# Routed slots in halves of 64: 36 token tiles in place of 39, three of them shared by two experts each

## What is computed

```python
def _swiglu(x, wg, wu, wd):                      # width 256 -> 512 -> 256
    return jax.nn.silu(x @ wg.T) * (x @ wu.T) @ wd.T
shared_out = _swiglu(x, shared_gate, shared_up, shared_down)
logits = x @ gate_w.T
top_id = jnp.argmax(logits, axis=-1)
score = jax.nn.sigmoid(jnp.max(logits, axis=-1))
xs = x * score[:, None]
def body(acc, ws):
    wg, wu, wd, e = ws
    xe = jnp.where((top_id == e)[:, None], xs, 0.0)
    return (acc + _swiglu(xe, wg, wu, wd), None)
...
x = x + 0.5 * ffn(layernorm(x))
x = x + attention(layernorm(x))
x = x + 0.5 * ffn(layernorm(x))
```

## Time and profile before

| | us |
|---|---|
| median of 3 runs | 1135.99 |
| lowest, highest | 1130.5, 1139.51 |
| the profiled execution, its own time | 1137.43 |
| its span, first to last instruction | 1135.5 |
| TensorE busy in it | 1096.2 |

### The profile page before, as it was taken

One profiled execution on the slowest core, in us unless ns is written; L12 is line 12 of the kernel. 1 busy time (PEld: TensorE's weight loads), 2 busy tenths in 40 slices (PEclk: granted clock), 3 DMA queues, 4 the chain that ended last, 5 costly groups with the idle time before them and its releaser, 6 DMA issues.

```text
span 1135.5 us, 30299 instructions
## 1 busy us (share of the span) xinstructions
PE 1096.2 (97%) x11410; PEld 891.7 (79%) x11411; DVE 764.8 (67%) x1411; ACT 582.7 (51%) x961; POOL 550.8 (49%) x764
## 2 busy tenths in 40 slices
PE   8999999999999889999999999989999999999997
PEld 6788888888888767677777777768888888888886
DVE  5736656767677487868878878755447477677674
ACT  4344336666666345555555555243433256666663
POOL 5720644676666553444543541327202726566664
PEclk8999999999999989999999999999999999999999
DMA  7273134222211220000000000105241232122220
GB/s 259 74 292 117 37 116 173 66 67 71 66 61 45 65 89 3 3 3 3 3 3 3 3 3 3 39 3 212 101 152 38 102 140 68 62 67 62 71 65 14
DMA packets 39472, 80.25 MB, mean 71 GB/s; under 512 B 6452, under 2 KB 31159, under 8 KB 38336
## 3 DMA queue, kind: packets, MB, share of 16 engines
q1 hardware_dynamic: 27568, 52.94, 12.9%
q0 software_dynamic: 11232, 25.20, 7.1%
q10 hardware_dynamic: 560, 0.52, 0.1%
HBM read 57.13 MB, written 27.00 MB: 74 GB/s over the span
## 4 chain that ended last, share of the span: by engine, by line
PE 80%; DVE 11%; ACT 4%; issue 2%; POOL 1%; DMA 1%; ACTq 0%; DVEq 0%; SPq 0%; POOLq 0%
PE PS L1851 19%; PE PS L1765 13%; PE PS L1865 12%; PE PS L1781 8%; PE PS L1858 3%; PE PS L1939 3%; PE PS L1696 2%; DVE A_NM L801 2%; PE PS L2059 2%; PE PS L1799 2%; PE PS L2072 2%; DVE A_NM L808 1%; ACT XNT L1272 1%; PE PS L1792 1%; PE PS L2010 1%
## 5 line engine op out<-in xcount | busy, mean ns | idle before, releaser
L1851 PE MATMUL PS<-WHL,XGH 128*128 128x512 f32 x624 | 217.5, 430 | 0.6 <-DVE WHL L682 0.6
L1865 PE MATMUL PS<-WD,XNT 128*128 x624 | 149.5, 382 | 1.5 <-ACT XNT L1191 1.5
L703 DVE SCALAR_TENSOR_TENSOR XNT<-PS,SCORES,XNT 128x512 f32<-128x512 f32 x78 | 58.6, 751 | 117.4 <-PE PS L1851 117.4
L1599 POOL TENSOR_TENSOR A_W<-A_XC,CB 128x256 f32<-128x256 f32 x86 | 61.7, 737 | 151.4 <-DVE A_XC L906 151.4
L1186 ACT ACTIVATE XNT<-PS,SCORES 128x512 f32<-128x512 f32 x78 | 53.8, 690 | 145.2 <-PE PS L1851 145.0
L1851 PEld LDWEIGHTS PS<-WHL,XGH 128*128 128x128 f32 x624 | 111.4, 189 | 18.8 <-DVE WHL L682 1.1
L1865 PEld LDWEIGHTS PS<-WD,XNT 128*128 128x128 f32 x624 | 112.6, 190 | 15.6 <-issue 2.0
L1506 POOL DMA_INDIRECT X<-xs_dram,WHO x78 | 96.5, 1238 | 57.6 <-issue 23.1
L1851 PE MATMUL PS<-WHL,XGL 128*128 128x512 f32 x312 | 123.2, 395 | 0.0
L1500 POOL TENSOR_SCALAR XNT<-WD 128x128 f32<-128x128 f32 x64 | 52.4, 838 | 128.9 <-DVE WD L576 128.9
L1781 PE MATMUL PS<-SDH,HHL 128*128 128x256 f32 x512 | 104.0, 287 | 1.7 <-DVE X L616 1.3
(11 more groups left out here) (280 smaller groups left out, 2555.1 us busy)
## 6 DMA issues: line engine op xcount, KB each, us to landing
xs_dram<-WG SPq DMA_DIRECT2D x16, 512.0 KB, 3.0
WU<-in_r_up SPq DMA_DIRECT2D x2, 4096.0 KB, 14.3
shared_dram<-X SPq DMA_DIRECT2D x16, 512.0 KB, 2.9
WG<-in_r_gate SPq DMA_DIRECT2D x2, 4096.0 KB, 16.7
WD<-in_r_down SPq DMA_DIRECT2D x4, 2048.0 KB, 8.2
X<-in_x SPq DMA_DIRECT2D x7, 512.0 KB, 9.6
X<-mid_dram SPq DMA_DIRECT2D x7, 512.0 KB, 3.9
X<-xs_dram,WHO POOLq DMA_INDIRECT x78, 3.0
```

The costliest lines, as they stand in the source:

```text
L703: dve.scalar_tensor_tensor(B["RH"][:, u * F:(u + 1) * F], banks[3 + u][:], score(t), B["RS"][:, u * F:(u + 1) * F], ALU.mult, ALU.mult).th ...
L1599: pool.tensor_tensor(B["W"][:].rearrange("p (a m) -> p a m", m=M)[:, part, :], B["XC"][b % 2][:].rearrange("p (a w) -> p a w", w=XW)[:, pa ...
L1851: ins = pe.matmul(banks[bank][:], tok, w[:, k * F:(k + 1) * F], start=(k == 0 and i == 0), stop=(k == KD - 1 and i == 2))
L1865: ins = pe.matmul(banks[7][:, 0:D], B["HT"][:, u * F + f * P:u * F + (f + 1) * P], B["WD"][:, bass.ds(ex * (KF * D) + f * D, D)], start=(f ...
```

## The change

Slots are given out in halves of 64. An expert with n tokens gets whole tiles, and one half more where the rest is at most 64 (otherwise the rest takes a whole tile). At most (4096 + 8 x 63) / 64 = 71 halves are needed, so 36 tiles: 33 full ones with one expert each and 3 "halved" ones (numbers 33 to 35) whose two halves of 64 slots have an expert each. EXPERT gets 39 entries: 33 for the full tiles, 6 for the halves. The three halved tiles are worked at positions 29, 32 and 35 of 36, so that the last nine positions are written out on all engines ("closing_tile").

In a halved tile the tokens are not split: ScalarE copies them once as plain float (xgt_whole), and no weights are cast. TensorE does gate and up with plain-float products, for each of the two halves of the width one product for each expert: 64 tokens as the stationary operand, 512 columns of weights moving, output to partitions 0 to 63 or 64 to 127 of the same bank. Down is done likewise, eight products of 64 x 256. The first expert's weights are read from WG, WU, WD in place, the second's from a buffer (SECOND) that SyncE fills from memory for each halved tile. The routing gets a step place_halves in slot 19 and one more operation in slot_numbers; counting starts a slot earlier and the two counting products come behind the slot's down products; find_experts moves from slot 26 to slot 27, ahead of read_table.

```diff
-SLOT_TILES = (T + E * (P - 1)) // P
+HALF_P = P // 2
+HALVES = (T + E * (HALF_P - 1)) // HALF_P
+SLOT_TILES = -(-HALVES // 2)
 UNR = 3
+FULL_TILES = SLOT_TILES - UNR
+PAIRED = 2 * UNR
+ENTRIES = FULL_TILES + PAIRED
...
+    FIRST_HALVED = SLOT_TILES - UNR * UNR
+    def halved(p):
+        return p >= FIRST_HALVED and p % UNR == UNR - 1
+    def fulls(p):
+        return p if p < FIRST_HALVED else p - (p - FIRST_HALVED) // UNR
...
-    COUNT_SLOT = 17
-    ROUTING_SLOT = dict(choose=14, one_hot=15, count_first=17, count_rest=18, count_tiles=19, slot_numbers=20, slot_places=21,
-                        tile_hot=22, owners=23, scores=24, find_experts=26, read_table=27)
+    COUNT_SLOT = 16
+    ROUTING_SLOT = dict(choose=14, one_hot=15, count_first=16, count_rest=17, count_tiles=18, place_halves=19, slot_numbers=20, slot_places=21,
+                        tile_hot=22, owners=23, scores=24, read_table=27)
...
+        half_at = PARTS_G * GT * D
+        B["SECOND"] = dict(WG=X[:, half_at:half_at + KD * F], WU=X[:, half_at + KD * F:half_at + 2 * KD * F], WD=B["HB"][:, 0:KF * D])
...
+            need(sp, "x_out_last", 16 * (NG - PARTS_G))
+            for i in range(UNR):
+                p = FIRST_HALVED + i * UNR + UNR - 1
+                if i > 0:
+                    need(sp, "ru", p - UNR + 1)
+                entry = FULL_TILES + 2 * i + 1
+                ex = sp.value_load(B["EXPERT"][0:1, entry:entry + 1], min_val=0, max_val=E - 1)
+                need(sp, "wg", 16 * (i + 1))
+                sp.dma_start(B["SECOND"]["WG"], r_gate[:, bass.ds(ex * (KD * F), KD * F)]).then_inc(s["wg"], 16)
+                need(sp, "wu", 16 * (i + 1))
+                sp.dma_start(B["SECOND"]["WU"], r_up[:, bass.ds(ex * (KD * F), KD * F)]).then_inc(s["wu"], 16)
+                if i == 0:
+                    need(sp, "dn", KF * NG)
+                else:
+                    need(sp, "ry_ready", p - UNR + 1)
+                need(sp, "wd", 32 + 16 * i)
+                sp.dma_start(B["SECOND"]["WD"], r_down[:, bass.ds(ex * (KF * D), KF * D)]).then_inc(s["wd"], 16)
...
+            def place_halves():
+                then(dve.scalar_tensor_tensor(odd, tiles, float(P), total, ALU.mult, ALU.is_lt))
+                then(dve.tensor_tensor_scan(odd_so_far, const("ones")[:, 0:E], odd, 0.0, ALU.mult, ALU.add))
+                then(dve.tensor_scalar(backward, odd_so_far, float(PAIRED), float(2 * SLOT_TILES + PAIRED), ALU.max, ALU.subtract))
+                then(dve.tensor_tensor(backward, backward, odd_so_far, ALU.add))
+                then(dve.scalar_tensor_tensor(to_half, ends, 2.0, backward, ALU.mult, ALU.add))
+                then(dve.tensor_tensor(rt1, banks[3][:, 0:NT * E].rearrange("p (t e) -> p t e", e=E), rt1, ALU.add))
+                then(dve.scalar_tensor_tensor(rt3, over_t(tiles), float(P), rt1, ALU.mult, ALU.is_le))
             def slot_numbers():
-                then(dve.tensor_tensor(rt1, banks[3][:, 0:NT * E].rearrange("p (t e) -> p t e", e=E), rt1, ALU.add))
+                then(dve.scalar_tensor_tensor(rt3, rt3, float(-HALF_P), over_t(to_half), ALU.mult, ALU.mult))
                 then(dve.scalar_tensor_tensor(rt1, over_t(starts), float(P), rt1, ALU.mult, ALU.add))
+                then(dve.tensor_tensor(rt1, rt1, rt3, ALU.add))
...
+            def closing_tile(p):
+                tile_hidden(p, p % UNR)
+                tile_ahead(p + 2)
+                if not halved(p):
+                    weights_ahead("WU", fulls(p) + 1, 1)
+                tile_out((p - 1) // UNR, (p - 1) % UNR)
+                if not halved(p):
+                    weights_ahead("WG", fulls(p) + 2, 0)
...
+            def xgt_whole(p, u):
+                need(act, "xg_t", p + 1)
+                act.copy(XNT[:, u * D:(u + 1) * D], banks[0][:, 0:D]).then_inc(s["xgt"], 1)
...
+            def through_halves(bank, p, w, ex, inc):
+                need(pe, w.lower(), 16 + 16 * (pair_of(p) + 1))
+                u = p % UNR
+                for k in range(KD):
+                    for h in range(2):
+                        at = u * D + k * P + h * HALF_P
+                        of = B["SECOND"][w][:, k * F:(k + 1) * F] if h else B[w][:, bass.ds(ex * (KD * F) + k * F, F)]
+                        ins = pe.matmul(banks[bank][HALF[h], :], XNT[:, at:at + HALF_P], of, start=(k == 0), stop=(k == KD - 1))
+                ins.then_inc(inc, 1)
+            def down_halves(p, ex):
+                need(pe, "ht_sb", p + 1)
+                need(pe, "ry", p)
+                need(pe, "wd", 32 + 16 * (pair_of(p) + 1))
+                u = p % UNR
+                for f in range(KF):
+                    for h in range(2):
+                        at = u * F + f * P + h * HALF_P
+                        of = B["SECOND"]["WD"][:, f * D:(f + 1) * D] if h else B["WD"][:, bass.ds(ex * (KF * D) + f * D, D)]
+                        ins = pe.matmul(banks[7][HALF[h], 0:D], B["HT"][:, at:at + HALF_P], of, start=(f == 0), stop=(f == KF - 1))
+                ins.then_inc(s["ry_ready"], 1)
...
-            for it in range(1 + (TILES3 - 2) // 2 * 2, TILES3 - 1):
-                for u in range(UNR):
-                    tile_tensor(it, u)
-            for u in range(UNR):
-                tile_tensor(TILES3 - 1, u, last=(u > 0))
+            for p in range(FIRST_HALVED, SLOT_TILES):
+                closing_tile(p)
```

More of the change, by code:

```diff
@@ L533, in ffn_vector @@
             total = B["RT2"][:, (NT - 1) * E:NT * E]
-            tiles, ends, starts = (B["CNT"][:, i * E:(i + 1) * E] for i in range(3))
+            tiles, ends, odd_so_far, starts, odd, backward, to_half = (B["CNT"][:, i * E:(i + 1) * E] for i in range(7))
+            ends_and_odd = B["CNT"][:, E:3 * E].rearrange("p (v e) -> p v e", v=2)
             def scan(e):
@@ L733, in ffn_vector @@
                     tile_vector(it, u, ex)
-            ex = [None] + [expert(SLOT_TILES - UNR + u) for u in range(1, UNR)]
-            for u in range(UNR):
-                tile_vector(TILES3 - 1, u, ex, ahead=UNR - 1 - u)
+            for p in range(FIRST_HALVED, SLOT_TILES):
+                closing_tile(p)
             tile_out(TILES3 - 1, UNR - 1)
@@ L1215, in ffn_scalar @@
                     tile_scalar(it, u, ex)
-            ex = [None] + [expert(SLOT_TILES - UNR + u) for u in range(1, UNR)]
-            for u in range(UNR):
-                tile_scalar(TILES3 - 1, u, ex, ahead=UNR - 1 - u)
+            for p in range(FIRST_HALVED, SLOT_TILES):
+                closing_tile(p)
             ht(SLOT_TILES - 1, UNR - 1)
@@ new lines, in tokens_ready, with closing_tile @@
+            def tokens_ready(p):
+                if halved(p):
+                    need(pe, "xgt", p + 1)
+                else:
+                    need(pe, "xgl", fulls(p) + 1)
+            def closing_tile(p):
+                u, past = p % UNR, p - 1
+                tokens_ready(p)
+                need(pe, "rsilu", p)
+                if halved(p):
+                    mine = expert(FULL_TILES + 2 * pair_of(p))
+                    through_halves(1 + u % 2, p, "WG", mine, s["rg"])
+                else:
+                    through(1 + u % 2, p, u, 0, s["rg"], fulls(p))
+                ht(past, past % UNR)
+                before = expert(FULL_TILES + 2 * pair_of(past) if halved(past) else fulls(past))
+                if halved(p):
+                    through_halves(3 + u, p, "WU", mine, s["ru"])
+                else:
+                    through(3 + u, p, u, 1, s["ru"], fulls(p))
+                if p + 2 < SLOT_TILES:
+                    tokens_ready(p + 1)
+                    xt((p + 2) // UNR, (p + 2) % UNR)
+                if halved(past):
+                    down_halves(past, before)
+                else:
+                    down(past, past % UNR, before)
```

140 lines of the change are left out of this document (89 added, 51 removed).

## The result

The changed kernel takes 1124.43 us, median of nine runs (1122.24 to 1128.45); the kernel before took 1134.2 on the same chip (nine runs, 1130.5 to 1139.51). The ratio is 0.9912, 95% interval [0.9896, 0.9927]: faster by 0.9%, where 2.1% was forecast (1112 us), and outside the range of 1104 to 1121. The profiled execution took 1124.68, span 1122.9, TensorE's granted clock 0.991.

A forecast was written before the change was run, and what follows sets the result against it. TensorE, busy 97% of the span, was taken to bound the kernel. 31.4 - 6.6 - 0.9 = 23.9 us off the profiled 1137.43 gave 1113.5, or 1112 us as a median; range 1104 to 1121.

The forecast's parts named there:

- Three tiles less: Routed stage: three tiles of 5.24 us removed, 15.7 us gained in each feed-forward, 31.4 us in both.
- Three halved tiles: TensorE's plain-float products, halves side by side, cost +1.1 us a halved tile, 6.6 us for six.
- rival (a): In halved tiles the two halves take turns: 6.3 us a halved tile, 1143 us; chance 0.08.
- (b): Weight loads stand open between groups in halved tiles: 2.1 us more a halved tile, 1125 us; chance 0.06.
- The second experts' weights: Three 512 KB transfers for each halved tile arrive before use: cost 0, cover 4.5 us at the least.
- rival (c): Second experts' weights come late for halved tiles, 3.5 us four times, 14 us more, 1126 us; chance 0.05.
- I count 0: Cost of the weight transfers sharing the engines with the gathers of tiles 1 and 2: 0 us.
- a bound of 2.8 us: Most a delayed gather of tiles 1 and 2 would cost, once a feed-forward: landing 8.0 less tile 5.24.
- The routing and the experts: Longer routing and later expert finding ahead of the routed stage: +0.43 us in each feed-forward, +0.9 in all.
- the longer routing: VectorE's added slot-number steps move GpSimd's row table to about 123.7 us, still in time for TensorE: cost 0.
- finding the experts: Moved behind the table and doubled in width, on the chain: +0.43 us each feed-forward, bounds 0 and 1.87.
- The sum: Whole kernel: 31.4 - 6.6 - 0.9 = 23.9 us gained, giving 1112 us.

The follow-up runs named there:

- number 4: Kernel before with 36 tiles in place of 39 and nothing else changed: 1113.1 us, ratio 0.9775.
- number 11: Changed kernel with the column halves in turn and both written to partitions 0 to 63: 1155.9 us, ratio 1.0172.
- number 1: Changed kernel with the first pair's three transfers of second experts' weights held back to tile 26: 1125.85 us, ratio 0.9874.
- number 12: Changed kernel with the first pair's transfers spread over tiles 6, 11, 16 and three more gathers in feed-forward 2: 1116.25 us, ratio 0.9817.
- number 6: Changed kernel with 54 semaphore increments padding GpSimd's program: 1129.31 us, ratio 0.995.
- 8: Kernel before with 36 tiles and 54 semaphore increments padding GpSimd's program: 1113.74 us, ratio 0.9818.
- number 9: Changed kernel with nine more small gathers that nobody reads, issued by GpSimd in feed-forward 2: 1127.81 us, ratio 0.9932.
- number 10: Changed kernel with the first pair's transfers spread over tiles 6, 11, 16 and nine more gathers in feed-forward 2: 1116.69 us, ratio 0.9829.
- number 7: Changed kernel with all chunks of one column half before those of the other in halved blocks: 1132.89 us, ratio 0.9965.

## Why the prediction was wrong

**Three tiles less: right.** 15.55 and 15.0 us for 15.7 (number 4).

**Three halved tiles: mechanism right, size 0.2 low.** The halves run side by side, in groups 0.43 us apart and so without open weight loads: rival (a) is priced at 5.1 us a tile by number 11, the 5.2 of the prediction (6.3 less 1.1), and is not what happens; (b) neither. The cost is 1.2 to 1.3 us a tile for 1.1. Gate takes 1.87 for 1.62 and up 1.87 for 1.48 (the earlier trace rows and the timeline below), a little less than forecast; not counted was the turn of the hidden rows between them, 0.58 for 0.36, which starts late behind plain-float halves as well.

```profile
331.20 0.64 PE L1983 MATMUL PS<-WG,XNT 128*64 x1
331.21 0.64 PE L1983 MATMUL PS<-X,XNT 128*64 128x512 f32 x1
331.68 0.59 PE L1983 MATMUL PS<-WG,XNT 128*64 x1
...
333.07 0.66 PE L1964 MATMUL PS<-CB,XNT 128*128 128x128 f32 x4
333.65 0.64 PE L1983 MATMUL PS<-WU,XNT 128*64 x1
```

Both together: 24.8 us forecast, 11.65 + 11.45 = 23.1 in the table.

**The second experts' weights: wrong, the step that failed.** It asked whether the transfers land in time for their users, and they do (no wait on them in the last nine tiles; rival (c) is out). What they do to others was put down as "I count 0", with a bound of 2.8 us. The bound takes them to meet the gathers of tiles 1 and 2, which have a tile of 5.24 us in hand. They meet those of tiles 0 and 1, and tile 0's combine had 1.8 us in hand. So the gather, late by 4.3 us, is felt: TensorE stands, comes back at the lower clock, and the late combine holds back GpSimd's queue and with it the next tokens. The bound has only the first of these. In the trace this costs 5.8 us in feed-forward 1, twice the bound. From trace to trace the size varies: over tiles 0 to 3 of feed-forward 1 the six traces with the burst are 3.5 to 6.2 us above the 15.60 of before, and seven without it lie at 15.53 to 17.15 (number 1, with its other hole, at 20.20).

**GpSimd's stops: not in the prediction at all.** Three tiles less also means nine indirect DMAs less in each feed-forward, and two stops of 3 us moved from covered places to the residual gather that opens feed-forward 2 and to the last scatter. They were in the trace before, at 372.7 us and at 1092.2: what lies beside TensorE can still be worth something by where it lies. At the end the stop costs 1.55 us; at the head of feed-forward 2 the stop and the burst share 4.0, and each alone would cost some 3 to 4.

**The routing and the experts: the sum right by luck.** Forecast were 0 for the longer routing and 0.43 us for finding the experts in each feed-forward, 0.9 in all. ScalarE's high part is at 157.34 for 156.92, 0.42 later. But VectorE's low part ahead of the experts is 0.34 later already (153.69 for 153.35), and behind it the high part comes only 0.08 later, in feed-forward 2 too. The first down block is 0.45 later in feed-forward 1, and in feed-forward 2 it comes 0.36 later behind the first shared product (167.64 for 167.28): 0.8 in all, for 0.9.

```profile
122.66 0.36 PE L1887 MATMUL PS<-SDH,HHL 128*128 128x256 f32 x1 [0.29 <-DVE X L679]
...
154.30 0.80 DVE L669 TENSOR_TENSOR WD<-CNT,CB 128x624 f32<-128x624 f32 x1
...
157.34 0.62 ACT L1235 CAST HHL<-HSB 128x512 fp32r<-128x512 f32 x1 [0.95 <-DVE HSB L686]
```

The 0.3 us come in slot 22. The work added to the slot numbers overruns VectorE's product by 0.33 (119.25 for 118.92), as forecast, and that sets back its output rows (L679), for which TensorE's down block now waits. The prediction followed the overrun only to GpSimd's row table, where it is covered. From slot 22 to slot 23 TensorE takes 4.76 us for 4.44 in both feed-forwards.

**The sum.** 23.9 forecast, 12.6 in the spans: 9.8 at the two heads, 1.55 at the end, 1.7 from the tiles, less 0.4 by which routing and experts were dearer in the forecast (0.9) than at the first down block of feed-forward 1 (0.45; what they cost in feed-forward 2 lies in the next term) and 1.3 that the two long stretches of the table, with the attention and with tiles 2 to 26, gave on balance. With the two holes closed (number 12) the span without the stretch to the first down block of feed-forward 2 is 24 us shorter than before, as much as was forecast, 0.9 of it at the end, where nothing was; its total is 20 us shorter (1136.72 to 1116.25), since that trace has 4.5 us more in that stretch, most of it in the attention.

**Open:** what GpSimd does in a stop, and what sets the exact place of the second; it does not hang on the place in its program (numbers 6 and 8). What stops three engines at the head of feed-forward 1 in number 1. Where the padding of number 6 loses 4 us. And whether the attention is a little longer in the changed kernel (514 to 521 us from the last down of feed-forward 1 to the table of feed-forward 2 in ten traces of it and its variants, 511 to 515.5 in four of the kernel before, two of these with 36 tiles) or only varies.

## What to carry to other kernels

A transfer that is "early enough" for its user still needs a place: look at what else is in flight when it starts, above all where a stage begins and no buffer is ahead, and spread it if it can be. When work is taken out, check what moves against what: fixed costs that lay under cover, here by a count of DMAs, come to lie elsewhere. And where removing a cause gives nothing, remove it together with the next suspect before calling it innocent: two causes that lie over each other each look cheap. A forecast that comes out right in its sum can still be wrong in both terms: compare each with its own stretch of the trace.

## What the hardware showed that was not expected

- GpSimd stops for 3.0 to 3.1 us behind its 113th indirect DMA since launch, at 372.7 us before, 922.5 after, 826.9 in number 9, 820.5 in number 10 and 901.0 in number 12, whatever the size of the gathers; a second one of 3.1 to 3.3 came 97 to 103 DMAs later.
- TensorE pairs up records of two column halves that are issued four apart (333.00 and 333.01 in number 7), so the order hardly matters for gate and up; down, eight apart, loses some 0.6 us a tile. On one half they take 3.58 us a block for 1.87.
- After a hole of 2.54 us a block of eight records took 3.50 us for 1.73, at a mean granted clock of 0.56.
- Three transfers of 512 KB issued within 1.5 us beside an indirect gather make its user wait 3.2 to 4.9 us, for 0.6 to 0.7 before; one at a time costs some 0.5 us or less.
